# Mixture-of-experts stage of an AdaLN block: tokens transposed after the second up block, six TensorE waits fewer per slot tile, weight pieces issued in a chain of their own

## The reference, cut to what matters

```python
logits = t @ switch_w + switch_b            # t: 4096 x 256
route_prob_max = jnp.max(softmax(logits)); routes = jnp.argmax(...)
for e in range(8):
    h = gelu(t @ w1[e] + b1[e])             # 256 -> 1024
    y = h @ w2[e] + b2[e]                   # 1024 -> 256
    out = jnp.where(routes == e, y, out)
x = x + gb * out * route_prob_max
```

## Time and profile before

| what | value |
|---|---|
| median of 3 runs | 800.48 us |
| the three runs | 801.36, 797.1, 800.48 us |
| span of the profiled execution, first to last instruction | 795.7 us |
| mean granted TensorE clock | 0.968 |
| TensorE matmul busy | 705.5 us (89%) |
| VectorE, ScalarE, GpSimd busy | 602.1, 502.3, 441.7 us |
| expert stage in the trace | 527 us to the end |
| first `up` matmul, last `down` matmul | 554.5 us, 783.6 us |

### The profile page before, as it was taken

One profiled execution on the slowest core, in us unless ns is written; L12 is line 12 of the kernel. 1 busy time (PEld: TensorE's weight loads), 2 busy tenths in 40 slices (PEclk: granted clock), 3 DMA queues, 4 the chain that ended last, 5 costly groups with the idle time before them and its releaser, 6 DMA issues. The chain is left out here.

```text
span 795.7 us, 20973 instructions
## 1 busy us (share of the span) xinstructions
PE 705.5 (89%) x7310; PEld 435.7 (55%) x7310; DVE 602.1 (76%) x1238; ACT 502.3 (63%) x1001; POOL 441.7 (56%) x577
## 2 busy tenths in 40 slices
PE   7868889999999999999999888674999999999993
PEld 5433444454554555445445443353777777777772
DVE  5767887988889889798898766347677777777774
ACT  1426778888888888888888888632444444444441
POOL 4403554777777877877877777823133434334321
PEclk8998999999999999999999999966999999999998
DMA  8105233244444734525535347358365655423000
GB/s 269 34 1 116 73 100 101 79 144 111 147 126 105 170 100 139 148 81 140 126 97 149 101 152 159 108 208 302 99 190 171 182 181 154 128 70 96 23 19 1
DMA packets 61364, 97.49 MB, mean 123 GB/s; under 512 B 8405, under 2 KB 42318, under 8 KB 60753
## 3 DMA queue, kind: packets, MB, share of 16 engines
q1 hardware_dynamic: 56272, 79.36, 33.9%
q0 software_dynamic: 4992, 16.79, 6.7%
HBM read 69.47 MB, written 34.51 MB: 131 GB/s over the span
## 5 line engine op out<-in xcount | busy, mean ns | idle before, releaser
L1115 DVE TENSOR_REDUCE row_max<-ps_max 128x2 f32<-128x768 f32 (+2 forms) x192 | 199.8, 1041 | 51.1 <-PE ps_max L652 51.0
L925 ACT ACTIVATE prob<-ps_sc 128x1024 f32<-128x1024 f32 (+1 forms) x192 | 169.2, 882 | 60.3 <-PE ps_sc L679 59.3
L1466 PE MATMUL ps_h<-tok_t,w_all 128*128 128x128 f16 x1872 | 156.5, 219 | 2.6 <-issue 2.0
L1466 PEld LDWEIGHTS ps_h<-tok_t,w_all 128*128 x1872 | 131.8, 98 | 44.4 <-issue 4.3
L433 POOL TENSOR_SCALAR_AFFINE_SELECT prob<-prob 128x512 f32<-128x512 f32 x128 | 82.2, 642 | 86.9 <-ACT prob L925 86.5
L1379 POOL DMA_INDIRECT slot_mem<-row_dram,token x39 | 46.2, 1184 | 139.6 <-DVE y L1676 119.6
L1536 ACT ACTIVATE hid<-ps_h,b_t 128x128 f32<-128x128 f32 x312 | 89.1, 372 | 50.1 <-PE ps_h L1466 50.0
L1480 PE MATMUL ps_y<-w_all,hid_parts 128*128 x312 | 118.5, 381 | 2.0 <-DVE hid_parts L1651 1.9
L692 PE MATMUL ps_pv<-prob,v_sb 128*32 128x512 f32 (+3 forms) x1024 | 88.8, 442 | 0.3
L645 PE MATMUL ps_max<-k_t,q_t 64*128 64x512 f16 (+3 forms) x512 | 68.5, 304 | 22.9 <-DVE row_max L1115 22.1
L1482 PE MATMUL ps_y<-w_all,hid_parts 128*128 x312 | 85.0, 273 | 0.0
(11 more groups left out here) (257 smaller groups left out, 1345.6 us busy)
## 6 DMA issues: line engine op xcount, KB each, us to landing
raw<-w SPq DMA_DIRECT2D x64, 256.0 KB, 3.0
w_dram<-halves SPq DMA_DIRECT2D x64, 256.0 KB, 3.3
w_all<-w_dram SPq DMA_DIRECT2D x20, 512.0 KB, 4.0
row_dram<-rows SPq DMA_DIRECT2D x32, 256.0 KB, 3.4
w_all<-w_dram SPq DMA_DIRECT2D x3, 2048.0 KB, 12.8
mod_rows<-mods_dram SPq DMA_DIRECT2D x16, 256.0 KB, 6.8
row_dram<-mods_dram SPq DMA_DIRECT2D x32, 128.0 KB, 4.6
xs<-x SPq DMA_DIRECT2D x24, 128.0 KB, 3.4
```

Source lines behind the costliest of these rows:

```text
L925: nc.scalar.activation(p_kb[:, :, first * L:(first + n) * L], ps_sc[:, :, 0:n * L], ACT.Exp, scale=SCALE).then_inc(exp_done, 1)
L1115: nc.vector.tensor_reduce(dst, ps_max[:, :, 0:n * L].rearrange("p j (m l) -> p j m l", m=n), AX.X, ALU.max).then_inc(max_done, 1)
L1466: last = mm(o, w[:, :, k, f, :][:, bass.ds(e, 1), :].rearrange("p e m -> p (e m)"), tok_t[:, j % 2, piece, k, :], start=(n == 0 and f % HF ...
```

## The change

The transposes of the next tile's tokens move from behind `up` f = 3 to behind `up` f = 1. Six of TensorE's eleven waits per tile go: `x_lo_done` at the transposes, `x_kept` and `gelu_done` at `up` f = 0, `gelu_done` at `up` f = 4, and `hi_done` at `down` f = 0 and f = 4. Each is implied by a wait that stays. The wait on `y_kept` at `down` f = 0 becomes one on `summed` (VectorE's second addition of the tile two before), so it is met earlier. The first call of `transposes(1)` gets an explicit wait on `x_lo_done`. The weight pieces wait only for the piece before, so they follow each other without a gap. `halves` gets an argument that nothing else uses.

```diff
+X_AT = 1
...
             for n in range(CHUNKS * (E - AHEAD)):
-                e, c, j = AHEAD + n // CHUNKS, n % CHUNKS, NB - 1 + n
+                e, c = AHEAD + n // CHUNKS, n % CHUNKS
...
-                sp.wait_ge(slot_loaded[j % NB], loads_before(j))
+                if c:
+                    sp.wait_ge(w_in[e], 16 * c)
                 sp.dma_start(w_all[:, e, c // (CHUNKS // 2), cols], w_dram[e, :, c // (CHUNKS // 2), cols]).then_inc(w_in[e], 16)
...
             def transposes(j):
                 pe.wait_ge(slot_loaded[j % NB], loads_before(j))
-                ge(pe, x_lo_done, j)
...
                 if f == 0:
-                    pe.wait_ge(x_kept, j + 1)
                     pe.wait_ge(x_lo_done, j + 1)
-                if f % HF == 0:
-                    ge(pe, gelu_done, 2 * (j - 2) + f // HF + 1)
...
                 if f % HF == 0:
-                    pe.wait_ge(hi_done, 2 * j + f // HF + 1)
                     pe.wait_ge(lo_done, 2 * j + f // HF + 1)
                 if f == 0:
-                    ge(pe, y_kept, j - 1)
+                    ge(pe, summed, 2 * (j - 1))
...
                 up(0, expert[0], f)
-                if f == HF - 1:
+                if f == X_AT:
+                    pe.wait_ge(x_lo_done, 1)
                     transposes(1)
...
                     up(j, expert[j], f)
-                    if f == HF - 1 and j + 1 < NJ:
+                    if f == X_AT and j + 1 < NJ:
                         transposes(j + 1)
                     down(j - 1, expert[j - 1], f)
...
-            def halves(j):
-                for q in range(2):
+            def halves(j, parts_of=(0, 1)):
+                for q in parts_of:
```

## The result

The changed kernel takes 789.51 us, the median of 4 runs (788.4 to 791.26); the kernel before took 799.21 us over its 4 runs (797.1 to 801.36). The ratio is 0.9892, with a 95% interval from 0.9866 to 0.9918: 1.1% faster. The forecast was 796.1 us (0.55% less), its range 793.2 to 800.8.

What follows compares the result with a forecast made beforehand. The prediction took TensorE's stream to bound the expert stage. Its terms, 4.6 + 0.6 - 0.9 + 0.5 - 0.4 = 4.4 us, came off the median of 800.48 to give 796.1 us, range 793.2 to 800.8.

Steps and rivals of the forecast that it cites:

- 32 ordinary steps: 4.6 us: TensorE's steps into f = 0 without a load or VectorE wait: from 0.811 to 0.667 us each, 4.6 us saved.
- 0.9 us given back: Five tiles with little margin behind VectorE's chain: TensorE waits there at down f = 0, losing 0.9 us of the gain.
- The four steps with a load: Steps into f = 0 holding a load of expert numbers: 0.144 us saved each, 0.6 us in all, bounds 0 and 1.2.
- scattered excess: Extra time in TensorE's other steps, some 1.4 us in all; its shrinking was counted only in a rival.
- more is won: Rival: load steps give 0.3 us each, scattered excess shrinks, no margin lost; 7.5 us saved, 793.0 us; chance 0.08.
- the excess at f = 0 is not the waits: Rival at TensorE's f = 0 step: new expert, bank or address calculation costs the time; 800.5 us; chance 0.24.
- my strict reading: TensorE's 64-deep queue puts its sequencer several steps ahead, so met waits cost nothing: 800.5 us, no change.
- VectorE becomes the bound in most tiles: Rival at down f = 0: VectorE's chain uses up the margin, 0.29 us against 0.2; 798.1 us; chance 0.18.
- margin of 0.15 us: Earlier transposes let gelu start sooner, giving VectorE's chain 0.15 us more margin in about half the tiles.
- The start: First down waits 0.56 us for VectorE; earlier tokens of tile 1 gain up to 0.5 us, a delayed first gather loses 0.4.
- The weight chain: Weight pieces following each other gain nothing by earlier arrival, but delay the first gather by 0.4 us, bounds 0 and 1.1.
- The slow rival: At tile 0's transposes: first gather lands late beside the weight pieces, 7.8 us delay, 803.9 us; chance 0.04.

Runs made afterwards that it cites:

- late wait alone: The changed kernel with the wait on hi_done given back at down f = 0 alone: 790.39 us, ratio 0.9883 to the kernel before.

## Why the prediction was wrong, point by point

- **"32 ordinary steps: 4.6 us" and "0.9 us given back".** Together 3.7 us were forecast and 4.37 + 0.02 came. The new step was put at 0.667 and is 0.66. Of the five tiles with little margin, the steps are 0.86, 0.80, 0.71, 0.73 and 1.16 after: 0.46 us of new waiting in four, where I had 0.65, and nothing more in the last, where I had 0.28. TensorE follows L1649 at 0.14 us there (749.70 to 749.84), not at the 0.2 I took as the least. The distance in the other tiles is 0.32 us and more, forecast 0.29 and up; the two ends of the stage, with 0.14, are apart. These terms held in size.
- **"The four steps with a load: 0.144 each, 0.6 us; bounds 0 and 1.2."** This is the first step that failed: 2.09 us. I charged a load step with what the waits at f = 0 seemed to cost. But a load stops the sequencer, for 0.65 to 0.66 us by the trace files (1.13 in the last), and what then shows is the stop less the lead. Before, without a lead, a load made the f = 0 step 0.65 to 0.70 us longer in the first three; after, only 0.26 to 0.36. With 4, 3, 2, 1 and 0 waits alone per tile the four load steps sum to 6.48, 5.88, 5.38 to 5.44, 4.39 to 4.67 and 3.93 us; the two kernels with more waits away from f = 0 (5.96, 6.04) show that they count from anywhere in the tile. The bound was too narrow because it looked only at the two instructions behind the load.
- **The other steps, left out of the sum.** This is the second: 2.00 + 0.17 us. I had formed the scattered excess, sized it at 1.4 us, and put it only into the rival "more is won" with a chance of 0.08; that rival as a whole, 7.5 us, was still too small. The excess is gone (179.33 to 179.44 us for these steps) from the kernels with at most two waits alone and the transposes behind f = 1, and all but 0.4 us of it from the two with the transposes behind f = 3 (179.69, 179.75). So most of it was missing lead, and the new order gives the last 0.3 to 0.4 us. The trace files bear this out. Apart from the transposes' step, 12 of these steps last over 0.69 us before, and 8 of them have one of the sequencer's longer stops (0.13 to 0.16 us) just ahead. After, there are more stops of over 0.1 us (37 against 27) and no such step. What makes the sequencer stop stays open.
- **The root of both** is that I took the rows (f = 0 has two such instructions, f = 4 has one and costs nothing visible) as a rule of the place. The same rows can be read as a budget of the tile, and that reading would have put the load steps and the scattered excess into the sum. The equal form at f = 4 led to the right number for f = 0 for the wrong reason.
- **The rival "the excess at f = 0 is not the waits"** (0.24) was wrong: waits dropped, excess gone. But the waits at f = 0 were not at fault more than the others. The Trainium skill (TensorE: Matmul & The Clock Gate, "Architectural detail: the array is 16x 32x32, not 1x 128x128") gives TensorE a queue 64 instructions deep. That met waits are then free was my strict reading and is not in the page. That reading agrees with the traces at up to two waits alone per tile (5.51 to 5.52 us) and not at three and more.
- **"VectorE becomes the bound in most tiles"** did not happen; TensorE's waits for it total 1.3 us in two, as before. It is nearer than that view shows. In the kernel "late wait alone" the wait for the low halves is an instruction of its own, and it lasts longer than the 0.05 us of a met one in 22 of 37 tiles; in all but five the lead covers that.
- **The transposes.** The mechanism showed as described, the worth is small: alone nothing, beside the waits 0.4 us of tile time (214.84 against 215.27), at the edge of what the traces tell. They keep the array busy for 0.22 us. Behind `up` f = 1 that restores the lead right after f = 0: the time from register instruction to matmul, taken at the `down` of f = 1, is 0.55 us (median) against 0.26 with the waits dropped alone. The margin of 0.15 us that the move was to give was hardly needed: with the waits dropped alone, VectorE's distance falls to 0.14 us in tile 4, whose step is 0.69.
- **The start** was put at 0.5 us gained and 0.4 us lost. From the first transposes to the first `down` it took 7.28 us before and 6.65 after, so 0.63 us were gained. The gather was not late in this execution (transposes 5.01 and 5.02 us behind its issue). But its issue came 0.60 us later (547.63 and 548.23), and so nothing was left of the gain. GpSimd's wait for the slot tables was 17.65 us before and 17.88 after; where the rest of the 0.60 comes from was not tried.
- **The weight chain** alone shows no cost in device time, and its one tile time is 0.34 us longer, which is no more than two traces differ. The slow rival (a late first gather) exists at a size of 0.9 to 1.7 us in some executions, not 7.8.

## What to carry to other kernels

When an in-order stream is shown 99% busy, divide it into its repeating steps and compare the period with the best step: matmuls per microsecond told here what the busy share hid. Count the instructions that only wait over a whole period, not where the loss shows, and drop implied ones until the array is the bound; beyond that they buy nothing but cover for rare stops such as a register load. If several parts of a change are bound together, run them apart: here one of three carried the gain.

## What the runs showed that I had not expected

An instruction that only waits, on semaphores long met, takes TensorE's sequencer 0.106 us. It lengthens the period by about 0.127 us once the lead is gone (5.66 us at four a tile, 6.04 at seven), by about 0.07 near the knee (5.52, 5.59, 5.66 at two, three and four), and not at all below. Behind a stop of the sequencer the price shows even where the period does not: two waits per tile instead of one lengthen each load step by about 0.2 us. The last load step is about 0.4 to 0.6 us longer than the other three in every version (2.01 against 1.50 before, 1.44 against 1.01 after). By the trace files the load instruction itself is longer: 1.07 us against 0.59 to 0.61 for the others, before and after alike. The last load reads seven numbers and the others eight; whether that is the reason was not tried.
